# Attention with routing in one software pipeline: another order on all four engines, and one exponential over four score banks

## The reference

```
xl = layernorm(x); xn = ln1(xl)
gate, clock, p, q, k, v = xn @ w_*            # q and k also with swapped pairs (w_qs, w_ks) for the rotation
cum = clip(cumsum(softplus(-gate)...)); pcs = cumsum(exp(p - max p) * softplus(clock))
q = rotate(q) * scale_q(cum, pcs, norm q);  k = rotate(k) * scale_k(cum, pcs, norm k)
a = exp(q @ k.T / sqrt(8)), causal;  o = (a @ v) / sum(a)
x1 = xl + o @ w_o;  x2 = x1 + gelu(ln2(x1) @ w_up) @ w_down
```

## Time and profile before

| | |
|---|---|
| median of 3 runs | 2470.77 us (2466.68 to 2477.46) |
| the profiled execution: time, span | 2465.03 us, 2463.3 us |
| PE, DVE, ACT, POOL busy, share of the span | 78%, 70%, 61%, 45% |
| mean granted clock of TensorE | 0.900 |
| attention's part of the span | about 43 to 1045 us |

### The profile page before, as it was taken

The page is one execution under the profiler, slowest core; times in us unless marked ns, Lnnn a source line. Parts: engine busy times, 40 slices in busy tenths (PEclk is TensorE's granted clock), DMA queues, the critical chain, the costliest instruction groups (busy, mean ns, idle before and its releaser), DMA issues. The chain is left out here.

```text
span 2463.3 us, 40082 instructions
## 1 busy us (share of the span) xinstructions
PE 1930.4 (78%) x12634; PEld 980.3 (40%) x12661; DVE 1726.9 (70%) x3563; ACT 1493.2 (61%) x2916; POOL 1102.2 (45%) x702
## 2 busy tenths in 40 slices
PE   3678887777887876199648889899888898775997
PEld 0345454444544443199612223332322222223443
DVE  4655655655656532257608999999999999994875
ACT  1576666666766653077535676666666666535875
POOL 0112111212121101158727788888888888860000
PEclk7899899999999986599878999999999999877998
DMA  3010000000100000122110000000000000003432
GB/s 136 18 31 23 23 23 23 27 23 25 37 23 19 19 14 22 31 64 85 68 39 15 25 22 22 22 21 21 21 21 21 21 30 17 18 9 101 100 82 73
DMA packets 98864, 88.51 MB, mean 36 GB/s; under 512 B 8416, under 2 KB 85392, under 8 KB 98336
## 3 DMA queue, kind: packets, MB, share of 16 engines
q1 hardware_dynamic: 91936, 68.52, 9.7%
q0 software_dynamic: 6784, 18.10, 2.2%
HBM read 38.01 MB, written 27.61 MB: 27 GB/s over the span
## 5 line engine op out<-in xcount | busy, mean ns | idle before, releaser
L1790 POOL TENSOR_TENSOR hc<-h,c_rep 128x1024 f32<-128x1024 f32 x256 | 602.1, 2361 | 179.3 <-DVE h L1772 173.1
L1772 DVE TENSOR_TENSOR_SCAN h<-decay,bank 128x1024 f32<-128x1024 f32 x256 | 585.4, 2287 | 30.3 <-DVE bank L1763 11.2
L1666 ACT ACTIVATE decay<-bank,neg_a_r 128x510 f32<-128x510 f32 x512 | 322.7, 683 | 271.5 <-PE bank L1552 271.3
L1538 PE MATMUL bank<-u_in,sel_rows 32*128 32x512 f32 x1024 | 322.8, 682 | 110.3 <-DVE h L1772 109.0
L1763 DVE TENSOR_TENSOR bank<-bank,b_rep 128x1024 f32<-128x1024 f32 x256 | 309.2, 1208 | 62.4 <-remote 51.9
L1552 PE MATMUL bank<-delta,sel_rows 32*128 32x512 f32 x1024 | 348.0, 684 | 1.5 <-ACT decay L1666 1.5
L662 ACT ACTIVATE es<-bank 128x384 f32<-128x384 f32 x512 | 210.1, 502 | 120.6 <-PE bank L467 120.5
L1011 POOL DMA_INDIRECT rows_in_dram<-row,idx x64 | 66.4, 1037 | 424.5 <-DVE row L954 409.9
L1538 PEld LDWEIGHTS bank<-u_in,sel_rows 32*128 32x128 f32 x1024 | 88.1, 195 | 306.8 <-DVE h L1772 263.9
L442 PE MATMUL bank<-xt,w_a 128*128 128x512 f32 x224 | 138.9, 713 | 70.4 <-DVE rot_b L820 32.5
L1567 PE MATMUL bank<-hc,y_sel 128*32 128x512 f32 x1024 | 151.3, 667 | 0.0
(11 more groups left out here) (334 smaller groups left out, 4185.3 us busy)
## 6 DMA issues: line engine op xcount, KB each, us to landing
r_tw<-r_o_t SPq DMA_DIRECT2D x96, 128.0 KB, 2.3
xvs<-xv SPq DMA_DIRECT2D x16, 512.0 KB, 2.9
xs<-rows_in_dram SPq DMA_DIRECT2D x72, 68.0 KB
w<-in_w_dram SPq DMA_DIRECT2D x2, 2048.0 KB
x_in<-in_x_dram SPq DMA_DIRECT2D x16, 256.0 KB
xlb_dram<-xl SPq DMA_DIRECT2D x16, 256.0 KB
xlb_m<-xlb_dram SPq DMA_DIRECT2D x16, 256.0 KB
x_m<-in_x_dram SPq DMA_DIRECT2D x16, 256.0 KB
```

The costliest lines, as they stand in the source:

```text
L1538: last = pe.matmul(BD[n % 2][:, i * STEP:(i + 1) * STEP], sel[at:at + 32, r, :], u_in[p if n < NS else q][at:at + 32, hf, :], start=True, ...
L1666: act.activation(decay[n % 4][:, i, :, 1:], seq(DL[i])[:, :, 1:], ACT.Exp, scale=c["neg_a_r"][:, hf, g:g + 1]).then_inc(s["n_da"], 1)
L1772: dve.tensor_tensor_scan(flat(h[n % RING]), decay[n % 4].rearrange("p i b t -> p (i b t)"), BD[n % 2], 0.0, ALU.mult, ALU.add).then_inc(s[ ...
L1790: pool.tensor_tensor(hc[n % RING][:, :, :], h[n % RING][:, :, :], c_rep[p][:, :].unsqueeze(1).to_broadcast([P, 2, STEP]), ALU.mult).then_i ...
```

## The change

Five things. (1) The four masks of a quad give one signal at the last (`s_score` counts 8 a pair, no more 32). (2) `exps` is one activation of 128x1536 over the four banks, into one tile `es`, where it was four of 128x384. (3) PE's, ACT's and DVE's lists of a step are in another order. (4) On DVE compound pieces are cut up so that others can stand in between: `heads_out` into `heads_rec` and `heads_o`, the statistics into `bn_stats` and `bn_aggr`, the rotation into three passes, and the routing's chain into single instructions. (5) On POOL the first pass of `xl` stands ahead of the wait for `f_nb`. No arithmetic is added or left out, and the transfers are the same.

```diff
-        es = [sb(f"es{n}", [P, 3 * P]) for n in range(8)]
+        es_all = sb("es", [P, 2, HS, 3 * P])
+        es = [es_all[:, n // HS, n % HS, :] for n in range(8)]
...
-                    pe.matmul(diag, c["ident_b"][:, :], c["mask_b"][:, :, :], start=False, stop=True,
-                              skip_group_check=True).then_inc(s["s_score"], 1)
+                    last = pe.matmul(diag, c["ident_b"][:, :], c["mask_b"][:, :, :], start=False, stop=True,
+                                     skip_group_check=True)
+                last.then_inc(s["s_score"], 1)
...
             def exps(n, u):
-                for st in range(HS):
-                    act.wait_ge(s["s_score"], u * 32 + HS * n + st + 1)
-                    if st == 0:
-                        since(act, s["s_av"], u * 8 + n - 1)
-                    last = act.activation(es[(n % 2) * HS + st][:, :], RING[st][:, 0:3 * P], ACT.Exp, scale=DH ** -0.5)
-                last.then_inc(s["s_exp"], 1)
+                act.wait_ge(s["s_score"], u * 8 + n + 1)
+                since(act, s["s_av"], u * 8 + n - 1)
+                scores = psum[:, 3 * 512:7 * 512].rearrange("p (s w) -> p s w", s=HS)[:, :, 0:3 * P]
+                act.activation(es_all[:, n % 2, :, :], scores, ACT.Exp, scale=DH ** -0.5).then_inc(s["s_exp"], 1)
...
+            if late:
+                weigh(5, k - 2, p)
+            if tail:
+                pe.wait_ge(s["m_h"], k - 2)
+                transposes(M, h_tok, s["m_ht"])
             if front:
                 pe.wait_ge(s["f_xt_sb"], k + 1)
                 since(pe, s["f_mk"], k)
                 project(FB, c["w_gate"], s["f_gate"])
             if tail:
-                pe.wait_ge(s["m_h"], k - 2)
-                transposes(M, h_tok, s["m_ht"])
+                pe.wait_ge(s["m_ht_sb"], k - 2)
+                up(0)
...
+            if tail:
+                act.wait_ge(s["m_ht"], k - 2)
+                since(act, s["m_up"], 4 * k - 12)
+                act.activation(h_t[:, :], M[:, :], ACT.Identity, scale=c["ln2_g"], bias=c["ln2_b"]).then_inc(s["m_ht_sb"], 1)
             if scores:
                 act.wait_ge(s["f_v"], k)
                 since(act, s["s_av"], 8 * k - 16)
                 act.activation(v_a[q][:, :, :, 0:DH], FA.rearrange("p (j h d) -> p j h d", j=TS, h=H), ACT.Copy).then_inc(s["f_vaug"], 1)
...
+            def heads_rec(i, u):
+                dve.wait_ge(s["s_tr"], u * 4 + i + 1)
+                dve.reciprocal(rec[:, :, :], AV.rearrange("q (n s w) -> q n s w", n=4, s=HS)[:, :, :, DH]).then_inc(s["s_rec"], 1)
+
+            def heads_o(i, u, par):
...
-                dve.wait_ge(s["s_tr"], u * 4 + i + 1)
+                dve.wait_ge(s["s_rec"], u * 4 + i + 1)
...
             if front:
-                pool.wait_ge(s["f_nb"], k + 1)
+                pool.wait_ge(s["f_rs"], k + 1)
+                since(pool, s["xlb_stored"], 16 * k)
+                pool.tensor_tensor(xl[:, :, :], x_in[p][:, :, :], of_tile(mv[p][:, :, 0]), ALU.subtract).then_inc(s["f_xl"], 1)
```

More of the change, by code:

```diff
@@ L523, in pe_step @@
             if tail:
[L524 to L527, removed]
+                pe.wait_ge(s["m_gelu"], 4 * k - 9)
                 up(3)
             if late:
-                quad(6, k - 2, p)
+                back(2, k - 2)
             if tail:
@@ L567, in pe_step @@
             if front:
[L568 to L571, removed]
+                pe.wait_ge(s["f_sq"], k + 1)
+                pe.wait_ge(s["f_ra"], k + 1)
+                pe.matmul(FA[:, :], c["ones_blk"], square[:, :], start=True, stop=True).then_inc(s["f_ssq"], 1)
             if tail:
@@ L592, in pe_step @@
                 last.then_inc(s["m_aff"], 1)
[L593 to L596, removed]
             if scores:
-                weigh(2, k - 1, q)
-            if scores:
-                weigh(3, k - 1, q)
+                weigh(1, k - 1, q)
+                quad(3, k - 1, q)
+                back(0, k - 1)
             if mid:
@@ L608, in pe_step @@
                 transposes(M, o_tok[p], s["m_ot"])
+            if front:
+                pe.wait_ge(s["f_ka"], k + 1)
+                pe.wait_ge(s["f_sk"], k + 1)
+                pe.matmul(FB[:, :], c["ones_blk"], square[:, :], start=True, stop=True).then_inc(s["f_ssk"], 1)
             if scores:
+                weigh(2, k - 1, q)
                 quad(4, k - 1, q)
+            if mid:
+                pe.wait_ge(s["m_ot_sb"], k - 1)
+                for j in range(TS):
+                    last = pe.matmul(M[:, j * P:(j + 1) * P], o_t[:, j * P:(j + 1) * P], c["w_o"], start=True, stop=True)
+                last.then_inc(s["m_ow"], 1)
             if tail:
@@ L624, in pe_step @@
                 last.then_inc(s["r_rank"], 1)
[L625 to L628, removed]
-                last.then_inc(s["m_ow"], 1)
             if scores:
+                weigh(3, k - 1, q)
+                quad(5, k - 1, q)
                 back(1, k - 1)
-                quad(5, k - 1, q)
             if front:
@@ L673, in act_step @@
                 act.activation(v_a[q][:, :, :, 0:DH], FA.rearrange("p (j h d) -> p j h d", j=TS, h=H), ACT.Copy).then_inc(s["f_vaug"], 1)
+            if late:
+                av_copy(2, k - 2)
             if tail:
[L675 to L677 removed]
                 since(act, s["m_dn"], k - 3)
[L679 to L685 removed]
@@ L686, in act_step @@
[L686 to L697 removed]
+                gelu(0)
@@ new lines, in act_step @@
+                gelu(1)
+                gelu(2)
+            if front:
+                act.wait_ge(s["f_pre0"], k + 1)
+                act.wait_ge(s["f_pre1"], k + 1)
+                since(act, s["f_soft"], k)
+                act.activation(mag[:, :, :], pre[:, :, :], ACT.Abs).then_inc(s["f_abs"], 1)
+            if tail:
+                gelu(3)
+                act.preload_act_table_set(EXP_LN)
+            if ln:
+                act.wait_ge(s["f_vv"], k + 2)
+                act.activation(vv[:, :, :], vv[:, :, :], ACT.Ln).then_inc(s["f_ln"], 1)
+                act.wait_ge(s["f_ln"], k + 2)
+                since(act, s["f_xl2"], k)
+                act.activation(rs[q][:, :, :], vv[:, :, :], ACT.Exp, scale=-0.5).then_inc(s["f_rs"], 1)
@@ L884, in dve_step @@
                 centred(h_tok, x2, mv_m, rs_m, s["m_yn"])
+            if front:
+                dve.wait_ge(s["f_ra"], k + 1)
+                dve.wait_ge(s["f_rb"], k + 1)
+                dve.tensor_tensor(rot[:, :], rot[:, :], rot_b[:, :], ALU.add).then_inc(s["f_rq"], 1)
+            if tail:
                 dve.wait_ge(s["m_yn"], k - 2)
```

358 lines of the change are left out of this document (190 added, 168 removed).

## The result

The changed kernel takes 2286.97 us (median of 4, 2283.34 to 2288.7) where the kernel before took 2471.93 on the same chip: a ratio of 0.925, interval 0.9225 to 0.9274.

The account below looks back on a forecast made before the run. No engine is full; waits between four in-order queues set the step. Waits 114.6 plus clock 23 minus 14 gave 124 us, plus 8 at the ends 132: 2470.8 - 132 = 2338 us, own range 2305 to 2375, eight-in-ten range 2305 to 2395.

Parts of the forecast that it names:

- The walk: One full step of the new order timed from profile durations; it closed at 43.0 us.
- The 13 steps: Attention from k_m's copy 2 to copy 15, 711.6 us before; predicted to gain 124 us.
- The exponential: ScalarE's one pass of 128x1536 over four banks: predicted 1.50 us, costing nothing where other TensorE work covers it.
- the signal: One signal for a quad's four masks: given no gain; the skill's estimate was 79 ns a quad, 10 us over 128.
- Fill and drain: Steps 1, 2 and 16 gain four avs waits of 1.89 us, 8 us; steps 17 and 18 give nothing.
- what it can't see: Roundings and small handovers in the 13 full steps, left as a cost of 14 us.
- o_tok: TensorE's weigh waiting for VectorE's division, 34.7 us in the 13 steps: 10.4 stay, 24.3 go.
- the issue waits: TensorE's waits at the loop's branches: three of 10.8 us become four of 3.6, so 3.6 us more.
- busy time, which fell: TensorE's work in the 13 steps, 564.32 us, 35.7 of it from lower clock; 23 us predicted to come back.
- waits worth 44.6 us: The back transposes waiting for ScalarE's copy of the weighted sums in the 13 steps; all 44.6 us go.
- 32.5 more: The projection w_k waiting for VectorE's rot_b in the 13 steps; all 32.5 us go.
- Nothing comes of it: Rival for the whole kernel: the waits reappear under other names, 2471 us; chance 0.04.

Follow-up runs that it names:

- e2_order: The changed kernel with four exponentials of 128x384 and four signals again, new order kept: 0.9289 of the kernel before.
- e3_ends: The kernel before with the one exponential, and the new order only in steps up to 2 and from 16 on: 0.9837 of the kernel before.
- e14_fill_dve: The changed kernel with VectorE's front part of steps 0 and 1 in the old order: 0.9351 of the kernel before.
- e16_fill_both: The changed kernel, up to step 1 with VectorE's front part in old order and ScalarE's square of k late as before: 0.9364 of the kernel before.
- e12_undo_backs: The changed kernel with transposes back 0 and back 1 ahead of quads 3 and 5 again: 0.9498 of the kernel before.
- e6_backs: The kernel before with only the four back transposes moved behind the quad each stood ahead of: 0.9947 of the kernel before.
- e10_noloop: The changed kernel with every attention step written out, so without the loop's branches: 0.9276 of the kernel before.

## Why the prediction was off, step by step

**What held.** The mechanism, each of its waits, and the size of the middle. The walk closed a step at 43.0 us; the steps ahead of the loop take 42.8 and those at the branches 47.1 to 48.8, where 48 was predicted. The 13 steps gained 130.4 for a predicted 124. The exponential (1.45 for 1.50) and the signal cost nothing that shows in this order (e2_order). On the first the Trainium skill, "ScalarE: Activation LUTs", section "What ACT_TABLE_LOAD costs", gave an estimate of 1.47 us, and the trace agrees with 1.446.

**The step that failed is "Fill and drain".** Its term was 4 x 1.89 = 8 us; the profile has 41.1 in attention outside the 13 steps, and e3_ends 37. The prediction priced one sort of wait, avs, in steps 1, 2 and 16, and declared steps 17 and 18 worth nothing. I had walked the full step and not the first ones. Steps 1, 2 and 16 were shortened by 9.8, 10.2 and 11.7 us, as much as a full step was (130.4 / 13 = 10.0), and step 17 by 6.7. Even of its own sort of wait the term had only the four longest: those for avs sum to 12.0 us in these three steps.

Walked as the middle was, the start shows VectorE's statistics, xn and TensorE's w_k 7 to 9 us earlier behind the copy of k_m in step 1. That the order of the end steps itself made the gain is shown by e3_ends. Which moves made it is shown in part: in steps 0 and 1 the places of VectorE's front part and of ScalarE's square matter (e14_fill_dve to e16_fill_both), but two of these runs add a wait of their own, and back 0 and 1 undone cost 3.8 us in steps 1 and 2 (e12_undo_backs). In step 16 the avs waits were 4.6 us, the waits for h_tok of 4.9 became 0.2, and 4.5 is busy time, at the higher clock. This rests on the two traces; no run took the last steps apart, except that with back 0 and 1 undone step 16 is 2.2 us longer.

**Terms that were off and nearly cancelled.** That the middle's waits came out right is partly luck. The walk left 14 us for "what it can't see", roundings and handovers; what came was something else, the wait for xl, 13 x 1.8 = 23.5, from a centring that takes 3.16 us, beside POOL's passes, where the walk had 1.1. Against it o_tok left 4.4 and not 10.4, and the issue waits stayed three, 9.1, and didn't become four, 14.4. The waits fell by 102.0 us, where the prediction had 114.6 - 14 = 100.6; the other 5.5 of the 6 us are busy time, which fell by 28.5 and not 23.

**What the sum rests on.** The prediction added waits up, 114.6 us, and checked the sum against a walk. The runs show that only the walk was evidence. Taken one by one, waits worth 44.6 us bought 0.5% (e6_backs), and 32.5 more made it slower. The rival "Nothing comes of it", to which I gave 0.04, is what each part does alone. It fails for the whole order, of all engines; which of the further moves make the difference no run isolates.

**The size that is left.** 2338 - 2287 = 51 us: 33 from the ends, 6 from the middle, 10 in unchanged code between these two executions, and the rest in the medians. Without those 10 the time, as an estimate, would be near 2297, still below the prediction's low end of 2305. (By its own terms its ends are 2471 - 162 = 2309 and, for a step of 47.5 us, 2369; it wrote 2305 and 2375.)

## What to carry over

Where four in-order queues hold each other, a row of waits says where an order is tight and not what a move is worth: write down the whole new step with times from rows and see where it closes, and expect one move alone to gain nothing or to lose. Walk the first and the last steps too: here each of them gained about as much as a full step. Put every engine into the walk, also one that nobody waits for: POOL's two passes fell into a pause of VectorE's before, and met its work in the changed order and in e6_backs, at 2 us a step. In a tuned order a small undoing (one centring some 5 us later, for which TensorE never waits) can cost more than its own wait.

## What the runs showed of the hardware

First, some passes of VectorE over data in SBUF stretch while POOL works. In e6_backs the four centrings of xn take 3.22 us, and those of h_tok, which follow when POOL is done, 1.11:

```profile
237.63 3.22 DVE L826 TENSOR_SCALAR xn<-x_in,f_mean_var,f_rstd 128x128 f32<-128x128 f32 x4
240.77 1.11 DVE L826 TENSOR_SCALAR h_tok<-x,m_mean_var,m_rstd 128x128 f32<-128x128 f32 x4
```

with POOL at the same time on:

```profile
237.90 1.26 POOL L1004 TENSOR_TENSOR mag<-mag,one_up 128x512 f32<-128x512 f32 x1 [10.87 <-ACT one_up L725]
239.25 1.27 POOL L1006 TENSOR_TENSOR log<-log,mag 128x512 f32<-128x512 f32 x1
```

Over the 13 steps of e6_backs, the 36 centrings of xn that run beside a pass of POOL take 1052 ns in the mean, the other 12 take 334. POOL's passes take 1.26 and 1.27 us, as they do before. VectorE's busy time of the 13 steps is 454.8 us in e6_backs where the kernel before has 428.2, and 25.4 of the 26.6 are in xn. An order also decides which passes meet POOL's, and that cost is in no row of waits by its name: in e6_backs it stands as the wait for xn, in the changed kernel as the wait for xl. The Trainium skill, "SBUF — State Buffer", section "SBUF: two separate sides", has a port pair that the two share and that, for some kinds of instructions, one of them holds for a whole instruction; the rows here agree with it, but no run tried the pair by itself.

Second, ScalarE reads four score banks in one instruction at 1.446 us for 1536 columns, less than the 1.64 of the four, so the bank edges cost nothing that shows.

Third, in the changed kernel the same wait of 1.8 us for xl is followed by the full clock in the steps ahead of the loop and by a lower one later. TensorE in the step from 589.46 us, with a projection of 1.71 us where one takes 1.02:

```profile
616.75 0.66 PE L435 MATMUL bank<-consts,xl 128*128 128x128 f32 x4 [1.80 <-DVE xl L808]
...
620.39 1.71 PE L431 MATMUL bank<-xt,w_a 128*128 128x512 f32 x2
```

That is the 1.6 us between the 42.8 and 44.4 of a step. e10_noloop has the full clock (1.00 over the 13 steps) and steps of 44.3, with the idle time ahead of h_t in its place. Why the two exchange stays open.
